# A four-layer graph network on one core: the attention's nodes finished in three stretches, and the source list loaded behind each batch of edge gathers

## The reference

```
x = layernorm(x + attention(x, src, dst))     # softmax over the edges of each destination
x = layernorm(x + mean_propagation(x, 3))     # three rounds of neighbour means
x = layernorm(x + edge_mlp_max(x, edge_attr)) # per edge an MLP, then a max for each destination
x = layernorm(x + norm_propagation(x, 3))     # three rounds, scaled by the root of the degree
```

```
aij  = (h_dst - h_src) @ (w2_W.T @ a) + a.w2_b
aexp = exp(aij - max over the edges of dst)
out  = sum(aexp * (h_src @ w2_W.T + w2_b)) / sum(aexp) + feat @ w1_W.T + w1_b
```

## Time and profile before

| what | us |
| --- | --- |
| runs of the kernel before (three), median | 14325.05 |
| lowest and highest of them | 14324.3 and 14400.83 |
| the profiled execution's own time | 14359.44 |
| the span in its trace | 14357.7 |
| the slot stage: first gather of edges to the first step of the next stage | 73.23 to 343.57 |
| the finish of the attention: first gather to the end of the last step on DVE | 5317.18 to 5532.87 |

### The profile page before, as it was taken

One profiled execution on the slowest core, in us unless ns is written; L12 is line 12 of the kernel. 1 busy time (PEld: TensorE's weight loads), 2 busy tenths in 40 slices (PEclk: granted clock), 3 DMA queues, 4 the chain that ended last, 5 costly groups with the idle time before them and its releaser, 6 DMA issues. The chain is left out here.

```text
span 14357.7 us, 254566 instructions
## 1 busy us (share of the span) xinstructions
PE 8012.0 (56%) x99382; PEld 6554.0 (46%) x99382; DVE 7383.5 (51%) x8080; ACT 4852.9 (34%) x7120; POOL 8443.8 (59%) x7325
## 2 busy tenths in 40 slices
PE   2555555555555545988862344444444434488987
PEld 2444444444444434988861111111111111488987
DVE  4666666666666656666751222222222222666666
ACT  1444444444444433655540000000000000355655
POOL 5777777777777771313136666666666666331313
PEclk7555555555555557999986666666666666799999
DMA  5222223232323225989871222222222222598988
GB/s 92 82 85 89 86 87 89 86 90 86 89 84 90 89 71 202 350 318 332 331 245 41 55 54 58 57 58 55 56 56 56 58 53 58 189 328 319 351 305 285
DMA packets 1047494, 1997.20 MB, mean 139 GB/s; under 512 B 327105, under 2 KB 645527, under 8 KB 1047311
## 3 DMA queue, kind: packets, MB, share of 16 engines
q1 hardware_dynamic: 587603, 1664.35, 31.4%
q0 software_dynamic: 235776, 185.47, 8.3%
q10 hardware_dynamic: 224060, 146.71, 4.1%
HBM read 1617.67 MB, written 381.43 MB: 139 GB/s over the span
## 5 line engine op out<-in xcount | busy, mean ns | idle before, releaser
L652 POOL DMA_INDIRECT attend_and_count_rows<-table,attend_and_count_ring x3136 | 3927.9, 1253 | 1076.4 <-issue 1001.2
L1352 POOL DMA_INDIRECT judge_edges_src_rows<-table,judge_edges_ring x3136 | 3023.8, 964 | 1536.6 <-issue 955.9
L1201 POOL DMA_INDIRECT base<-slot_sums,last_slot x588 | 995.2, 1693 | 2977.8 <-DMA slot_sums<-propagate_mean_whole 1406.8
L687 PE MATMUL attend_and_count_counts<-attend_and_count_hot_hi,attend_and_count_hot_lo 128*128 128x98 bf16 x15680 | 1442.0, 270 | 2321.8 <-ACT attend_and_count_stage L796 1420.2
L687 PEld LDWEIGHTS attend_and_count_counts<-attend_and_count_hot_hi,attend_and_count_hot_lo 128*128 128x128 bf16 x15680 | 1191.7, 133 | 2571.2 <-ACT attend_and_count_stage L796 1400.6
L796 ACT CAST attend_and_count_stage<-attend_and_count_counts 128x784 uint8<-128x784 f32 x1960 | 1531.8, 812 | 897.5 <-PE attend_and_count_counts L687 536.3
L1108 PE MATMUL propagate_mean_p_dense<-propagate_mean_split,propagate_mean_part 128*128 128x96 bf16 x36456 | 1662.0, 208 | 303.4 <-ACT propagate_mean_part L1005 233.2
L1108 PE MATMUL propagate_norm_p_dense<-propagate_norm_split,propagate_norm_part 128*128 128x96 bf16 x36456 | 1663.2, 208 | 243.3 <-ACT propagate_norm_part L1005 169.1
L1108 PEld LDWEIGHTS propagate_mean_p_dense<-propagate_mean_split,propagate_mean_part 128*128 128x128 f16 x36456 | 1638.5, 100 | 311.2 <-ACT propagate_mean_part L1005 233.3
L1108 PEld LDWEIGHTS propagate_norm_p_dense<-propagate_norm_split,propagate_norm_part 128*128 128x128 f16 x36456 | 1641.4, 100 | 251.2 <-ACT propagate_norm_part L1005 170.0
L1489 ACT ACTIVATE judge_edges_hidden<-judge_edges_p_hid,judge_edges_b 128x512 f32<-128x512 f32 x392 | 247.7, 685 | 4236.8 <-remote 3145.4
(11 more groups left out here) (262 smaller groups left out, 12025.1 us busy)
## 6 DMA issues: line engine op xcount, KB each, us to landing
propagate_mean_raw<-matrix SPq DMA_DIRECT2D x372, 1568.0 KB, 8.8
propagate_norm_raw<-matrix SPq DMA_DIRECT2D x372, 1568.0 KB, 8.8
matrix<-attend_and_count_stage SPq DMA_DIRECT2D x245, 784.0 KB
scan<-attend_and_count_out SPq DMA_DIRECT2D x196, 272.0 KB
inject<-attend_and_count_zeros SPq DMA_DIRECT2D x49, 1024.0 KB
attend_and_count_rows<-table,attend_and_count_ring POOLq DMA_INDIRECT x3136
judge_edges_src_rows<-table,judge_edges_ring POOLq DMA_INDIRECT x3136
judge_edges_dst_rows<-inject SPq DMA_DIRECT2D x195, 256.0 KB
```

The lines of the kernel that those rows point to most:

```text
L652: nc.gpsimd.indirect_dma_start(out=rows[:, u, g, j, :], out_offset=None, in_=D.table0[:, :], in_offset=rows_of(ring[:, u, g, j:j + 1])).th ...
L687: last = nc.tensor.matmul(counts[:, r % 2, k // 4, NH * (k % 4):NH * (k % 4) + NH], hot_lo[:, u, slot, :], hot_hi[:, u, slot, :], start=Tr ...
L1201: nc.gpsimd.indirect_dma_start(out=sums[:, h, :], out_offset=None, in_=D.slot_sums[0:blocks * BLOCK, :], in_offset=rows_of(S.last_slot[:, ...
L1352: nc.gpsimd.indirect_dma_start(out=src_rows[:, u, lane, :], out_offset=None, in_=D.table2[:, :], in_offset=rows_of(ring[:, u, lane:lane + ...
```

## The change

The source list: the 11 pieces are written out and no longer a loop. Pieces 0 to 3 wait for batch 0 of the edge gathers, pieces 4 to 7 for batch 1, pieces 8 to 10 for batch 2. The rest follows them without a wait of its own.

The finish of the attention: DVE makes, once for all 98 columns and ahead of the first wait for a gather, what the three borders need, in five steps for each border: the test for both nodes is now two operations in place of three, and the border's maximum is kept in `side`. The maximum over the borders is kept in the new tile `reach`. Then the columns are handled in three stretches of 42, 42 and 14 (`STRETCHES`). A stretch waits for the gathers of all the slices in it, takes the larger of the gathered maxima and `reach` in one step, and goes on as a slice did. POOL's gathers, their semaphores and their order are as they were. The counts at which later stages start follow the new number of stretches.

```diff
--- before.py
+++ after.py
@@ -51,6 +51,7 @@
 N_BATCHES = SLOT_COLS // SLOT_BATCH
 SLICE = 14
 SLICES = [slice(first, first + SLICE) for first in range(0, NH, SLICE)]
+STRETCHES = [slice(0, 3 * SLICE), slice(3 * SLICE, 6 * SLICE), slice(6 * SLICE, NH)]
 NEG = -1.0e30
 EPS = 1e-5
 Y0_ROW = FEAT + 2
@@ -479,10 +480,11 @@
 
             whole = N_EDGES // CHUNK
             piece = whole // SRC_PIECES
-            sp.wait_ge(gathered[1], 16 * B * (N_BATCHES // 2))
-            with sp.Fori(0, SRC_PIECES) as i:
-                sp.dma_start(S.src_all[:, bass.ds(i * (piece * LANES), piece * LANES)].rearrange("p (k j) -> p k j", j=LANES),
-                             D.src[bass.ds(i * (piece * CHUNK), piece * CHUNK)].rearrange("(k p j) -> p k j", p=P, j=LANES)).then_inc(src_loaded, 16)
+            for i in range(SRC_PIECES):
+                batch = min(i // 4, N_BATCHES - 1)
+                sp.wait_ge(gathered[batch % 2], 16 * B * (batch // 2 + 1))
+                sp.dma_start(S.src_all[:, i * piece * LANES:(i + 1) * piece * LANES].rearrange("p (k j) -> p k j", j=LANES),
+                             D.src[i * piece * CHUNK:(i + 1) * piece * CHUNK].rearrange("(k p j) -> p k j", p=P, j=LANES)).then_inc(src_loaded, 16)
             rest = (N_EDGES - whole * CHUNK) // LANES
             sp.dma_start(S.src_all[0:rest, whole * LANES:(whole + 1) * LANES],
                          D.src[whole * CHUNK:N_EDGES].rearrange("(p j) -> p j", j=LANES)).then_inc(src_loaded, 16)
@@ -883,6 +885,7 @@
     cut_dst = sb("cut_dst", [P, GROUPS - 1, 2], i32)
     cut_dst_f = sb("cut_dst_f", [P, GROUPS - 1, 2], f32)
     top = sb("top", [P, NH], f32)
+    reach = sb("reach", [P, NH], f32)
     side = sb("side", [P, GROUPS, NH], f32)
     other = sb("other", [P, NH], f32)
     total = sb("total", [P, NH], f32)
@@ -919,21 +922,24 @@
         def _(dve):
             dve.wait_ge(cuts, 32 * (GROUPS - 1))
             link(nc.vector.tensor_copy(cut_dst_f[:], cut_dst[:]))
-            for n, cols in enumerate(SLICES):
+            for g in range(GROUPS - 1):
+                link(nc.vector.tensor_scalar(other[:], S.node_id[:], cut_dst_f[:, g, 0:1], None, ALU.is_equal))
+                link(nc.vector.scalar_tensor_tensor(other[:], S.node_id[:], cut_dst_f[:, g, 1:2], other[:], ALU.is_equal, ALU.mult))
+                link(nc.vector.tensor_scalar(other[:], other[:], 1.0, -NEG, ALU.subtract, ALU.mult))
+                link(nc.vector.tensor_scalar(side[:, g], other[:], cut[:, g, FEAT + 1:FEAT + 2], None, ALU.add))
+                if g:
+                    link(nc.vector.tensor_tensor(reach[:], reach[:], side[:, g], ALU.max))
+                else:
+                    link(nc.vector.tensor_copy(reach[:], side[:, g]))
+            for n, cols in enumerate(STRETCHES):
+                many = cols.stop - cols.start
                 ends, one = last[:, cols], other[:, cols]
-                dve.wait_ge(gathered[n], 16 * SLICE)
-                link(nc.vector.tensor_copy(top[:, cols], ends[:, :, FEAT + 1]))
-                for g in range(GROUPS - 1):
-
-                    link(nc.vector.tensor_scalar(one, S.node_id[:, cols], cut_dst_f[:, g, 0:1], None, ALU.is_equal))
-                    link(nc.vector.tensor_scalar(side[:, g, cols], S.node_id[:, cols], cut_dst_f[:, g, 1:2], None, ALU.is_equal))
-                    link(nc.vector.tensor_tensor(one, one, side[:, g, cols], ALU.mult))
-                    link(nc.vector.tensor_scalar(one, one, 1.0, -NEG, ALU.subtract, ALU.mult))
-                    link(nc.vector.tensor_scalar(side[:, g, cols], one, cut[:, g, FEAT + 1:FEAT + 2], None, ALU.add))
-                    link(nc.vector.tensor_tensor(top[:, cols], top[:, cols], side[:, g, cols], ALU.max))
+                for m in range(cols.start // SLICE, cols.stop // SLICE):
+                    dve.wait_ge(gathered[m], 16 * SLICE)
+                link(nc.vector.tensor_tensor(top[:, cols], ends[:, :, FEAT + 1], reach[:, cols], ALU.max))
                 link(nc.vector.tensor_copy(side[:, GROUPS - 1, cols], ends[:, :, FEAT + 1]))
                 sided.append(link(nc.vector.tensor_tensor(side[:, :, cols], side[:, :, cols],
-                                                          top[:, cols].unsqueeze(1).to_broadcast([P, GROUPS, SLICE]), ALU.subtract)))
+                                                          top[:, cols].unsqueeze(1).to_broadcast([P, GROUPS, many]), ALU.subtract)))
                 dve.wait_ge(weighed, n + 1)
                 own, sums, whole = side[:, GROUPS - 1, cols], S.work[:, cols], total[:, cols]
                 link(nc.vector.tensor_tensor(whole, ends[:, :, FEAT], own, ALU.mult))
@@ -941,7 +947,7 @@
                 for g in range(GROUPS - 1):
                     link(nc.vector.scalar_tensor_tensor(whole, side[:, g, cols], cut[:, g, FEAT:FEAT + 1], whole, ALU.mult, ALU.add))
                     link(nc.vector.tensor_tensor(part[:, cols], over_features(side[:, g, cols]),
-                                                 cut[:, g, 0:FEAT].unsqueeze(1).to_broadcast([P, SLICE, FEAT]), ALU.mult))
+                                                 cut[:, g, 0:FEAT].unsqueeze(1).to_broadcast([P, many, FEAT]), ALU.mult))
                     link(nc.vector.tensor_tensor(sums, sums, part[:, cols], ALU.add))
                 link(nc.vector.reciprocal(one, whole))
                 link(nc.vector.tensor_tensor(one, one, S.has_edges[:, cols], ALU.mult))
@@ -976,7 +982,7 @@
     splitted, summed_parts, spread, kept, stored, *gathered = S.group_sems
     first = turn * ROUNDS
     v = sem(name + "_vector_step")
-    root = (turn + 1) * (len(SLICES) + 1)
+    root = len(STRETCHES) + 1 + turn * (len(SLICES) + 1)
     steps = [0]
 
     def place_of(k, b, u):
@@ -1535,7 +1541,7 @@
     b2_loaded = sem("finish2_b2_loaded")
     gathered = S.slice_gathered
     v = sem("finish2_vector_step")
-    root = len(SLICES) + 1
+    root = len(STRETCHES) + 1
     steps = [0]
 
     def link(ins):
```

## The result

The changed kernel took 14257.0 us (median of 7 runs, 14199.15 to 14290.09), the kernel before, beside it, 14339.55 (median of 7). The ratio is 0.9934 with a 95% interval of 0.9917 to 0.9951: 82.6 us less between the medians, 70 to 119 by the interval. The profiled execution took 14257.0 us, its span is 14255.3.

What follows compares the result with a forecast made beforehand. No one engine bounds the kernel (none above 59% busy); DVE ends both changed stages. Finish 50.1 us plus slot stage 2.6 us gave 52.7 less, from the median 14325.05 to 14272.3; range 14245 to 14340.

Steps and rivals of the forecast that it cites:

- a measurement tells only some 1% (143 us) from no change: Whole kernel: timing resolves some 1%, 143 us; "same" got 0.96, faster and slower 0.02 each.
- The slot stage: End of the slot stage: moving the list's loads saves 2.6 us, bounds 0 and 2.6, as DVE is next to finish.
- the 60 us that the page seems to promise: Slot stage after the last gathers: DMA full with the list looks like 60 us, but only the last 3 wait.
- The moved loads: Slot stage's batches of edge gathers: list pieces loaded among them cost nothing; without cover up to 56 us.
- The finish, the work: Attention's finish: 26 steps a stretch, 26.4 us for 42 columns, 12.7 for the third; 65.5 us in place of 119.
- The push: Attention's finish: wide operations in stretch 1 hold gathers and push gather 84 back by 7 us, bounds 0 and 22.
- the Trainium skill's rule as I put it: Finish's gathers: tensor_tensor takes only the read interface, so would hold no gather; by it the sum is 7 us better.
- The slow pace: Attention's finish: DVE steps 1.40 us apart beside gathers were taken to recur at the same place; stage 50.1 us less.
- Against: nothing in the change takes away its place: Attention's finish: argument against the pace not returning, since it stays beside POOL's gathers and ACT's exponentials.
- The rival "does not return": Attention's finish: no slow pace in the changed kernel, 60.7 + 2.6 us less, 14261.7; chance 0.17.
- the same frame: Sign for the pace not returning: the other finish, with like gathers, steps and roots, ran at full pace.
- The rival on the slower side: Attention's finish: slow pace belongs to the profiled execution alone, so 9 us more, 14334; chance 0.2.

Runs made afterwards that it cites:

- e5: The kernel before, unchanged, measured against itself on a quick chip (some 13490 us): ratio 0.9994, finish 145.0 us.
- e11: Border steps made once, seven slices kept, list's loads moved, against the kernel before on a late chip: ratio 0.9935, finish 167.2 us.
- e13: Three stretches, each making its 18 border steps itself, list not moved, against the kernel before on a late chip: ratio 0.9965, finish 166.9 us.
- e16: The changed kernel with four stretches (42, 28, 14, 14 columns) against the kernel before on a late chip: ratio 0.9969, finish 148.3 us.
- e9: The kernel before, unchanged, measured against itself on a late chip (14330 to 14430 us): ratio 0.9994, finish 212.8 us.
- e12: The kernel before plus seven trial stages behind its output (DVE step chains, alone or beside gathers or table loads), late chip; no ratio given.
- e15: The kernel before plus five trial stages behind its output (DVE or ACT chains beside gathers, plain loads or memsets), late chip: finish 213.4 us.
- e17: The kernel before plus four trial stages behind its output (DVE chains of small or mixed steps beside 98 gathers), late chip; no ratio given.
- e14: The changed kernel plus 41 idle operations (65 us) behind its finish, against the kernel before on a late chip: ratio 1.0011, finish 213.2 us.
- e10: The changed kernel, unchanged, against the kernel before on a late chip: ratio 0.9924, finish 147.9 us.
- e7: Border steps made once, seven slices kept, list's loads moved, against the kernel before on a quick chip: ratio 0.9956, finish 140.5 us.
- e1: The list's loads moved alone, old finish kept, against the kernel before on a quick chip: ratio 0.9977, finish 145.1 us.

## Why the prediction was right and wrong

**The number.** 14272 was said and 14257.0 measured, inside the range. That they lie so close is in part luck: 52.7 us less were said and 82.6 came, and the median of the kernel before rose by 14.5 us when it was taken of seven runs in place of three. Besides, the prediction held that a measurement tells only some 1% (143 us) from no change. This one told 0.66%: the interval ends at 0.9951 and is, with seven runs each, 0.17% to either side.

**The slot stage.** Right. 2.6 us were forecast and 3.1 came (1.8 to 4.0 in the other pairs); the 60 us that the page seems to promise were not there. The next stage follows DVE's last step. The moved loads cost nothing: the batches begin 55 us apart as in the earlier trace rows.

**The finish, the work.** Right. 26 steps a stretch, wide ones of 1.56 us as worked out from the earlier trace rows, stretches of 26.6 and 12.6 us for 26.4 and 12.7.

**The push.** The wide operations hold the gathers about as much as worked out, and the gate moved by half of it. At 1.25 us each, gather 84 would be issued 103.8 us behind the first. In the kernel after it was issued 110.1 us behind (5310.01 to 5420.14), so the wide operations ahead of it cost some 6 us, where I took 7. But the old steps held the gathers too: before, the same distance was 5423.58 - 5317.18 = 106.4 us, and 110.7 in e5, where the old finish ran at full pace. The sum left that out, and so the push against before was 3.7 us, inside 0 to 22. The gathers of 1.29 us and more beside wide operations speak against the Trainium skill's rule as I put it. The same section (SBUF — State Buffer, Who interferes with whom) also says that an operation of DVE with two inputs in SBUF contends with what GpSimd reads; with that sentence the trace agrees, if a gather counts as such a reader.

**The slow pace: the step that failed.** "I take 50, the same pace at the same place, since it is this stage's own". This is the term of 50.1 us in the sum, and the stage became 64.0 us shorter. The pace of 1.40 us was taken as given for the changed code, and it did not come: stretches 1 and 2 took 26.6 us each and not 46. It is neither the stage's own nor tied to its place. On late chips it comes when many short steps run beside gathers, and the changed finish has too few of them: 26 in 26.6 us, with 44 and 32 us of rest ahead of the first two stretches. "Against: nothing in the change takes away its place" looked at the place and not at the number of steps, which the change cuts from 308 to 93. e11 and e13 show that fewer steps and wider ones each take some 46 us off, and that it takes both together to keep the pace away; with a fourth stretch (e16) it is back. The rival "does not return" had 60.7 + 2.6 us, and the stages gave 64.0 + 3.1; it had a chance of 0.17 and should have had the forecast's.

The trace of before had a sign of this. The rival rests on the other finish, which ran at full pace beside the same 98 gathers, in "the same frame". The frame isn't the same where it counts: `finish_judging` has 13 steps to a slice and 10 to 11 us of rest behind each slice, where the old `finish_attention` has 44 and, at the slow pace, none. The table of stretches of the kernel before, for six of those slices, has 78 operations in 106 us and none 1.40 us apart; the earlier trace rows has 81 in 102 us at the slow pace, but there DVE always had the next of 44 steps at hand, and here it rested for want of gathers:

```profile
12256.00:12362.00 106.00, 0.00 (x0) 0.00 (x0) 40.97 (x78) 1.28 (x6) 81.16 (x81) 0.50 0.08 13
```

**The rival on the slower side.** Half of it was right. Without the slow pace the old finish does end 17 us behind the last gather, and the new one later: on the quick chips by 2.8 us where 11.6 was worked out (5472.2 - 5460.6). What was wrong is "the slow pace belongs to the profiled execution alone": the old finish has it in the profiles of e9, e12, e15 and e17 as in the first, on three late chips, and on neither quick one, and e14 shows its cost in the medians of the runs. One profile can't tell the one from the other; that the median stood only 34 us lower was fair evidence against the rival, whose pace costs 72.

**The surplus.** Between the medians the changed kernel gained 83 us in the first comparison and 99 in e10, where its two stages give 67 and 69, and the propagations of the profiles were 29 and 69 us shorter. The prediction has no term for this. e14 speaks against a property of the changed program, though the changed kernel without the idle work wasn't run on that chip. e7 (59 us less by the ratio, 6 in the stages), e1 (31 and 2) and e16, which misses the other way (45 and 68), show that ratios move by more than the stages and by more than their intervals. What moves the propagations from 1938 to 1998 us on the late chips is left open. So is `attend_and_count`, another untouched stage, with 4968 to 5012 us there and 4962 to 4965 on the quick ones.

## What to carry to other kernels

A pace that no instruction's duration explains is to be seen on a second chip before it is forecast: here the same program gains 0.7% or nothing, by the chip. Ask also whether the pace would be there without the recording; here that is open. When a slow stage is compared with a like one that is not slow, count the steps and the rests of both. Fewer and wider steps with rests between them kept the slow pace away here in the changed kernel; four stretches or 44 steps in each did not. The last gate should have little behind it. For a change of 0.3% the sum of the stages is a better guide here than the ratio, whose interval doesn't know how far an untouched stage wanders.
